# Layer norm and weight products of the node tiles moved ahead in the opening of a two-layer graph kernel

## The reference

```
h   = relu(layernorm(x))
A   = relu((adj + adj.T) / 2);  D = sum(A, axis=1);  d = D ** -0.5
x   = x + relu((I - d A d) @ (h @ W0))                 # layer 0
h   = relu(layernorm(x))
out = x + diag(adj) * (h @ W1[0]) + triu(adj, 1) @ (h @ W1[1])
        + tril(adj, -1) @ (h @ W1[2]) + bias           # layer 1
```

## Time and profile before

| | us |
|---|---|
| median of 3 runs (968.04 to 968.94) | 968.15 |
| the profiled execution | 966.95 |
| its span in the trace | 965.1 |
| first matmul of step 0 starts | 93.75 |
| PE busy | 915.6 (95% of the span) |
| DVE / ACT / POOL busy | 554.6 / 493.7 / 283.9 |

### The profile page before, as it was taken

One profiled execution on the slowest core, in us unless ns is written; L12 is line 12 of the kernel. 1 busy time (PEld: TensorE's weight loads), 2 busy tenths in 40 slices (PEclk: granted clock), 3 DMA queues, 4 the chain that ended last, 5 costly groups with the idle time before them and its releaser, 6 DMA issues.

```text
span 965.1 us, 17388 instructions
## 1 busy us (share of the span) xinstructions
PE 915.6 (95%) x4535; PEld 774.2 (80%) x4535; DVE 554.6 (57%) x1481; ACT 493.7 (51%) x1042; POOL 283.9 (29%) x284
## 2 busy tenths in 40 slices
PE   3657999999999999999999998999999999999998
PEld 2547788888888888888888887888888888888886
DVE  4896787777777776565656554543433433433442
ACT  2898466666666664555455554343333333333331
POOL 4783344344343443434434442111111100000000
PEclk9899999999999999999999999999999999999999
DMA  9996999999999985655565555676656655555552
GB/s 286 328 265 156 290 338 322 326 327 332 324 331 318 335 275 180 178 171 162 174 196 161 166 175 176 187 221 190 188 179 189 193 160 170 166 164 165 158 168 69
DMA packets 181689, 213.73 MB, mean 221 GB/s; under 512 B 13712, under 2 KB 116112, under 8 KB 179600
## 3 DMA queue, kind: packets, MB, share of 16 engines
q1 hardware_dynamic: 138928, 159.23, 54.6%
q10 hardware_dynamic: 42720, 54.01, 16.1%
HBM read 145.04 MB, written 68.16 MB: 221 GB/s over the span
## 4 chain that ended last, share of the span: by engine, by line
PE 88%; DVE 4%; ACT 2%; SPq 2%; DMA 1%; issue 1%; POOL 0%; DVEq 0%; ACTq 0%; POOLq 0%
PE psAcc L543 24%; PE psAcc L541 24%; PE psAcc L542 24%; PE psA L427 3%; PE psG L510 2%; PE psG L512 2%; PE psG L511 2%; PE psZ L469 2%; DVE sring L842 1%; DMA colb<-in_adj 1%; ACT hst L573 1%; SPq L236 1%; PE psW L396 1%; DVE n_st L797 1%; PE psW L395 1%
## 5 line engine op out<-in xcount | busy, mean ns | idle before, releaser
L607 ACT ACTIVATE Lh<-C 128x512 fp32r<-128x512 f32 x256 | 161.3, 631 | 293.4 <-PE psAcc L543 233.0
L541 PE MATMUL psAcc<-Xh,Lh 128*128 128x512 f32 x512 | 206.1, 402 | 0.7 <-DVE Xl L975 0.4
L541 PE MATMUL psAcc<-Yh,Lh 128*128 128x512 f32 x512 | 200.8, 392 | 0.0
L543 PE MATMUL psAcc<-Xh,Ll 128*128 128x512 f32 x512 | 200.7, 392 | 0.0
L542 PE MATMUL psAcc<-Xl,Lh 128*128 128x512 f32 x512 | 200.2, 391 | 0.0
L543 PE MATMUL psAcc<-Yh,Ll 128*128 128x512 f32 x512 | 200.1, 391 | 0.0
L542 PE MATMUL psAcc<-Yl,Lh 128*128 128x512 f32 x512 | 199.9, 390 | 0.0
L784 DVE TENSOR_TENSOR Ll<-C,Lh 128x512 fp32r<-128x512 f32 x128 | 90.8, 711 | 143.8 <-ACT Lh L607 143.7
L543 PEld LDWEIGHTS psAcc<-Xh,Ll 128*128 128x128 f32 x512 | 96.3, 188 | 20.8
L543 PEld LDWEIGHTS psAcc<-Yh,Ll 128*128 128x128 f32 x512 | 96.1, 188 | 20.3
L541 PEld LDWEIGHTS psAcc<-Xh,Lh 128*128 128x128 f32 x512 | 96.6, 189 | 18.8 <-issue 1.5
(11 more groups left out here) (125 smaller groups left out, 1380.4 us busy)
## 6 DMA issues: line engine op xcount, KB each, us to landing
C<-at_dram SPq DMA_DIRECT2D x128, 256.0 KB, 2.7
at_dram<-AT SPq DMA_DIRECT2D x16, 1088.0 KB, 5.5
R<-in_adj SPq DMA_DIRECT2D x64, 256.0 KB, 6.2
C<-in_adj SPq DMA_DIRECT2D x64, 256.0 KB, 5.2
s_dram<-C ACTq DMA_DIRECT2D x64, 256.0 KB, 5.0
g_dram<-g ACTq DMA_DIRECT2D x32, 512.0 KB, 3.6
C<-s_dram SPq DMA_DIRECT2D x64, 256.0 KB, 3.9
t_dram<-x ACTq DMA_DIRECT2D x32, 256.0 KB, 2.1
```

What stands on the lines that cost most here:

```text
L541: mm(acc, lh, rh[:, kd, :], start=k == 0, stop=False)
L543: mm(acc, ll, rh[:, kd, :], start=False, stop=c < L1 and k == NB - 1).then_inc(used, 1)
L607: A(Lh[:, q, :], C[:, q, :], ACT.Relu if s.c < L1 else ACT.Copy).then_inc(lhi, 1)
```

## The change

SP loads the first four node tiles between the four parts of strip 0, the weights after them, and the other twelve with strips 1 to 5 (three, three, three, two, one), each ahead of its strip. Stats, norm, turn and copy of the tiles stand in lists of their own and are placed in blocks behind chunks 3, 7, 11, 15 and 18. The turned tile is written back to `hst` instead of to four buffers. The weight products have three banks instead of two (`product0`: two of `psG` and `psZ`, the last tile in `psAcc`). The transposes of quarters 0 and 1 of step 0 stand behind chunks 35 and 37, the fourth quarter and the last three weight products behind the first quarter of step 0, and `xp` is turned at the end of step 0.

```
-        TILES_WITH = [2, 2, 2, 2, 1, 2, 1, 1, 2, 1, 0, 0, 0, 0, 0, 0]
-        TURN_AT = [8, 10, 15, 16, 21, 22, 27, 28, 31, 32, 35, 36, 37, 38, 39, 39]
-        SCALE_AT = [12, 13, 19, 20, 25, 26, 31, 32, 35, 36, 39]
+        TILES_WITH = [0, 3, 3, 3, 2, 1, 0, 0, 0, 0, 0, 0, 0, 0, 0, 0]
+        STAT_AT = [-1, 0, 1, 2, 3, 3, 3, 7, 7, 7, 11, 11, 11, 15, 15, 18]
+        MEAN_AFTER = [2, 4, 6, 8, 9, 12, 14, 15]
+        POWER_AT = [0, 2, 3, 7, 7, 11, 15, 18]
+        NORMAL_AT = [1, 1, 3, 3, 3, 3, 7, 7, 7, 7, 11, 11, 15, 15, 18, 18]
+        TURN_AT = [3, 3, 3, 3, 7, 7, 7, 7, 11, 11, 15, 15, 18, 18, 20, 20]
-        COLS_AT = [9, 16, 22, 28, 32, 36]
-        DEG_AT = [9, 17, 23, 29, 33, 37]
+        COLS_AT = [7, 15, 21, 27, 31, 35]
+        DEG_AT = [7, 15, 22, 28, 32, 36]
+        ROOT_AT = [7, 15, 21, 27, 31, 35]
+        TIMES_AT = [7, 7, 15, 15, 23, 24, 29, 30, 33, 34, 37, 38]
+        HIGH_AT = [7, 7, 15, 15, 24, 25, 30, 31, 34, 35, 38, 39]
+        LOW_AT = [8, 8, 16, 16, 26, 27, 32, 33, 36, 37]
...
-            return psZ[:, :] if j == 12 else psW[:, :] if j == 13 else psG[:, j % 2, :]
+            return psAcc[:, 1, :] if j == NB - 1 else psZ[:, :] if j % 3 == 2 else psG[:, j % 3, :]
...
+                    load_tiles([g])
                     sp.dma_start(rowb[:, 0, c], rows_v[k, :, c]).then_inc(ld_first[g], 16)
                     sp.dma_start(colb[:, 0, g * Q:g * Q + w * P].rearrange("p (j c) -> p j c", c=P),
                                  cols_v[k, :, 4 * g:4 * g + w, :]).then_inc(ld_first[g], 16)
-                    if g < TILES_WITH[0]:
-                        load_tiles([g])
+                load_weights()
...
     # times_W0, PE
-                if j == 13:
-                    pe.wait_ge(d_cols, len(GROUPS) - 1)
-                elif j != 12:
-                    done = j - 3 if j >= 14 else j - 1
-                    wait(pe, prep_hi, done)
-                    wait(pe, prep_lo, done)
+                if j < NB - 1:
+                    wait(pe, prep_hi, j - 2)
+                    wait(pe, prep_lo, j - 2)
...
     # chunk loop, PE
+                if n in (36, 39):
+                    pe.wait_ge(at_ok, 1 if n == 36 else 2)
...
+                for j in range(len(TIMES_AT)):
+                    if TIMES_AT[j] == n:
+                        times_W0(j)
                 for j in range(NB):
                     if TURN_AT[j] == n:
                         turn0(j)
+                if n in (35, 37):
+                    pe.wait_ge(p0S, 35 if n == 35 else 38)
+                    rows_T(Step(None, 0), 0 if n == 35 else 1)
+            columns0(len(GROUPS) - 1)
+            pe.wait_ge(p0S, len(CH0) - 1)
+            rows_T(Step(None, 0), 2)
             times_W0(12)
...
     # step 0, PE
-                if k == 11 and c < NB:
+                if k == (11 if c else 15) and c < NB:
...
+                    if c == 0 and q == 0:
+                        pe.wait_ge(p0S, len(CH0))
+                        rows_T(t, 3)
+                        times_W0(13)
+                        times_W0(14)
+                        times_W0(15)
...
     # chunk loop, ACT
-                for j in range(NB):
-                    if 2 * j + 6 == n:
+                for j in range(NB + 2):
+                    if j < NB and NORMAL_AT[j] == n:
                         normal0(j)
-                for j in range(NB):
-                    if TURN_AT[j] == n:
-                        turned0(j)
+                    if j >= 2 and TURN_AT[j - 2] == n:
+                        turned0(j - 2)
+                for j in range(len(HIGH_AT)):
+                    if HIGH_AT[j] == n:
                         scaled_hi(j)
...
     # chunk loop, DVE
+                stats_at(n)
+                for j in range(len(LOW_AT)):
+                    if LOW_AT[j] == n:
                         scaled_lo(j)
...
     # chunk loop, POOL
+                for e in range(len(ROOT_AT)):
+                    if ROOT_AT[e] == n:
+                        root(e)
                 for u in range(NB // 2):
-                    if 4 * u + 2 == n:
+                    if POWER_AT[u] == n:
```

More of the change, by code:

```diff
@@ L244, in load_first @@
                                  cols_v[k, :, 4 * g:4 * g + w, :]).then_inc(ld_first[g], 16)
-                    if g < TILES_WITH[0]:
-                        load_tiles([g])
+                load_weights()
             def load0(i):
                 k = NB - 1 - i
+                j = NQ + sum(TILES_WITH[0:i])
+                load_tiles(range(j, j + TILES_WITH[i]))
                 if i >= 3:
@@ L255, in load0 @@
                                  cols_v[k, :, 0:k, :]).then_inc(ld_col[i % 3], 16)
-                j = sum(TILES_WITH[0:i])
-                load_tiles(range(j, j + TILES_WITH[i]))
             def load_next(s, q):
@@ L285, in _ @@
                 load0(i)
-                if i == NB - 5:
-                    load_next(Step(None, 0), 0)
-            for q in range(1, NQ):
+                if i in (10, 12):
+                    load_next(Step(None, 0), i // 2 - 5)
+            for q in range(2, NQ):
                 load_next(Step(None, 0), q)
@@ L410, in times_W0 @@
                 pe.wait_ge(t0_ok, j + 1)
-                if j == 13:
-                    pe.wait_ge(d_cols, len(GROUPS) - 1)
-                elif j != 12:
-                    done = j - 3 if j >= 14 else j - 1
-                    wait(pe, prep_hi, done)
-                    wait(pe, prep_lo, done)
+                if j < NB - 1:
+                    wait(pe, prep_hi, j - 2)
+                    wait(pe, prep_lo, j - 2)
                 for b in range(HB):
                     f = slice(b * F, (b + 1) * F)
-                    last = mm(product0(j)[:, f], T0[j % 4][:, f], x1[:, 0, 0:F], start=True, stop=True)
+                    last = mm(product0(j)[:, f], hst[:, node(j), f], x1[:, 0, 0:F], start=True, stop=True)
                 last.then_inc(w0_ok, 1)
@@ L579, in turned0 @@
                 act.wait_ge(t0, j + 1)
-                wait(act, w0_ok, j - 3)
-                A(T0[j % 4], psAcc[:, j % 2, :], ACT.Copy).then_inc(t0_ok, 1)
+                A(hst[:, node(j), :], psAcc[:, j % 2, :], ACT.Copy).then_inc(t0_ok, 1)
             def scaled_hi(j):
@@ L827, in degrees, with stats_at @@
                                        op0=ALU.mult, op1=ALU.add).then_inc(d_safe, 1)
+            def stats_at(n):
+                for j in range(NB):
+                    if STAT_AT[j] == n:
+                        stats0(j)
+                        for u in range(NB // 2):
+                            if MEAN_AFTER[u] == j:
+                                mean0(u)
             def scaled_lo(j):
@@ L843, in _ @@
                                 rowb[:, (NB - 1 - k) % 3, 4 * g * P:4 * g * P + w], ALU.add).then_inc(p0S, 1)
[L844 to L849, removed]
                 for e in range(len(DEG_AT)):
@@ L852, in _ @@
                         degrees(e)
-                for j in range(len(SCALE_AT)):
-                    if SCALE_AT[j] + 2 == n:
+                stats_at(n)
+                for j in range(len(LOW_AT)):
+                    if LOW_AT[j] == n:
                         scaled_lo(j)
-            sum_T(Step(None, 0), 0)
+                if n in (36, 38):
+                    sum_T(Step(None, 0), 0 if n == 36 else 1)
+                if n == 38:
+                    split_lo(Step(None, 0), 0)
+            scaled_lo(10)
             degrees(len(GROUPS) - 1)
-            scaled_lo(10)
+            split_lo(Step(None, 0), 1)
             scaled_lo(11)
-            sum_T(Step(None, 0), 1)
-            split_lo(Step(None, 0), 0)
+            sum_T(Step(None, 0), 2)
             scaled_lo(12)
+            split_lo(Step(None, 0), 2)
+            sum_T(Step(None, 0), 3)
             scaled_lo(13)
-            sum_T(Step(None, 0), 2)
-            split_lo(Step(None, 0), 1)
             scaled_lo(14)
-            sum_T(Step(None, 0), 3)
+            split_lo(Step(None, 0), 3)
             scaled_lo(15)
-            split_lo(Step(None, 0), 2)
-            split_lo(Step(None, 0), 3)
             dve.wait_ge(d_inv, len(GROUPS))
```

57 lines of the change are left out of this document (16 added, 41 removed).

## The result

| | before | after | ratio |
|---|---|---|---|
| median, us | 968.1 (965.57 to 968.94, 4 runs) | 998.05 (997.36 to 999.58, 4 runs) | 1.0313 [1.0295, 1.0331] |
| span of the profiled execution | 965.1 | 997.9 | |
| step 0's first matmul | 93.75 | 122.83 | |
| from there to the end | 871.35 | 875.1 | |

The change makes the kernel 3.1% slower. The forecast was 991 us, in a range from 976 to 1000. The profiled execution, 999.58 us, is the longest of the four; the other three have spans of 995.6 to 996.6. So the trace after holds about 1.5 us that the median doesn't, and a difference between two traces can be off from that of the medians by as much.

What follows compares the result with a forecast made beforehand. ACT and DVE waits were taken to bound the opening, PE the 64 steps. Step 0 at 116 us plus 872.2 behind it gives span 988, 23 more than before; added to the median, 991 us, range 976 to 1000.

Steps and rivals of the forecast that it cites:

- the forecast's own sum: Whole kernel: step 0 starts at 109 to 119 us, so the span is 984 to 994; chance 0.62.
- the slow clock or further waits (994 to 1003): Whole kernel: half clock in step 0's first quarter, or more waits, gives 994 to 1003 us; chance 0.13.
- The weights: Start of opening: weights land behind strip 0 and four tiles, so the first chunk begins at 14.9 us, not 7.16.
- The blocks: Opening to chunk 22: waits followed block by block leave ACT idle 29.7 us and end at 93.6 us.
- The faster rival: Opening: blocks fill idle time, ACT idle only 6 us, step 0 at 85.4, time 960.6 us; chance 0.09.
- The rival with half the waits: Opening: 15 us less idle time, step 0 at 101, 976 us; case 972 to 984, chance 0.14.
- The tiles ahead of the strips: Early loads: strip 1 lands 3.9 us later, near 22.5, hidden since its first chunk is held until 36.
- The rest: From chunk 22 to step 0: 15.5 us of ACT work plus waits, step 0 taken at 116 us.
- my upper bound: Late opening: followed through degrees, ring, POOL's additions and chunk 36, step 0 starts at 118.5 us.
- The fixed part: From step 0's first matmul to the end: 2.34 us stall goes, 0.45 and 2.7 us are added, 872.2 us.
- The slow clock: Step 0's first quarter at half clock adds 2.8 us, 997 us; chance 0.13 shared with further waits.

Runs made afterwards that it cites:

- e1: The changed kernel with the two weight loads issued first, as before: 991.41 us, ratio 1.0234.
- e2: The kernel before with the two weight loads moved behind strip 0: 968.46 us, ratio 0.9994.
- e3: The changed kernel with stats, power and mean of tiles 7, 10, 11, 13, 14 and 15 one block earlier: 987.67 us, ratio 1.0197.
- e5: The changed kernel, loads and late part kept, with the chunk loop's stats, norms, turns, products and degrees back in their old places: 974.27 us, ratio 1.0057.
- e14: The changed kernel with the pairs one block earlier and the weights loaded first as well: 979.52 us, ratio 1.0112.
- e6: The changed kernel with the chunk loop's work back in its old places and the weights loaded first: 974.81 us, ratio 1.0065.
- e9: The kernel before with only the late part of the change; loads, weights and chunk-loop places as before: 967.76 us, ratio 0.9999.
- e10: The changed kernel with quarters 0 and 1 of step 0 behind the last chunk again: 997.49 us, ratio 1.0312.
- e13: The changed kernel with columns, degrees and roots of groups 3 to 5 one chunk later: 1001.58 us, ratio 1.0337.
- e4: The changed kernel with xp turned behind k = 11 of step 0 again: 1001.29 us, ratio 1.0342.
- e8: The changed kernel with xp turned behind k = 15 in step 1 too: 998.71 us, ratio 1.0315.

## Why the prediction was right, and where it was off

The measured 998.05 us lies inside the stated range, 2 us from its upper end, but above the 984 to 994 us that the forecast's own sum gave (chance 0.62). It fell in the next case, "the slow clock or further waits (994 to 1003)", which had 0.13, and by further waits. The direction, the cause and the chain through the blocks were forecast; that 998 was still inside owes something to a wide range.

**The weights.** Forecast 14.9 us for the first chunk, measured 15.23 on PE and 15.01 on ACT. That it counts nearly in full in this order is shown (e1: the relu of chunk 0 comes 8.2 us earlier, step 0 7.8 us, the median 6.6), and e2 shows that it is the order that makes it count.

**The blocks.** The chain followed held at nearly every point: `mean0` of pair 0 forecast at 23.3, measured end 23.34; end of the first block 39.4, measured 39.2; `mean0` of pair 3 at 47.2, measured 46.91; waits of ACT forecast as 5.4, 3.8, 4.8 and 3.1 us, measured as 5.44, 3.97, 5.66 and 3.53. ACT's idle time up to chunk 22, forecast as 29.7 us, is 30.8 (23.6 for the mean, 7.2 for DVE's chunks). That the late stats, power and mean of each pair's second tile cause most of these waits is shown by e3, which moves the three together; that the places as a whole are the main loss is shown by e5. The faster rival needed under 13.5 us of idle time on ACT; the waits for the mean alone are 23.6. The rival with half the waits (972 to 984) didn't hold; even e3, with the pairs in time, measured 987.67, and it took the weights first as well to come to 979.52 (e14).

**The tiles ahead of the strips.** "That is hidden, since its first chunk is held until 36": in the trace after, PE has no wait for a transfer between 16 and 100 us, so it held here, as a reading of waits and not by a run. In the old places it costs 6 to 7 us (e6 against e9). Along one order of undoing the terms are: loads ahead 6.7 (968.1 to 974.81, e6), blocks with the pairs in time 4.7 (to 979.52, e14), pairs late 11.9 (to 991.41, e1), weights late 6.6 (to 998.05). In another order they would have other sizes: the weights are worth 6.6 us here and nothing in the old places.

**The rest: the step that was off.** I took chunk 22 at 93.6 and 22.4 us from there to step 0, between bounds of 15.5 and 24.9. The relu of chunk 22 ends at 95.9, and from there it takes 26.9 us: 2.3 and 4.5 us more, and more than my upper bound. Of the 2.3, 1.1 was there when ACT's last block began (87.26, forecast 86.2). Then chunk 21 stood behind the last turns on PE at half clock, and chunk 22 waited for POOL. Of the 4.5 us behind it, about 3 are a term that I had sized too small, ACT's waits. I had given them 6.9 us beside 15.5 us of work; the view of ACT from 94 us to step 0 has

```profile
ACT sring L614 <- DVE sring L848: 10.8, 12, 2.0
```

of which about 10 lie behind chunk 22, beside about 17 us of work. DVE in turn mostly waits for PE, and for PE the views above show waits that I had not priced: 2.5 us for POOL ahead of the columns, and 1.4 us for a strip that I had "just in time". e10 and e13 show that neither the quarters between the chunks nor the columns' place can be taken out for a gain: another wait stands close behind each. So the size is measured; that its cause is a set of near ties rather than one wait is what these two runs suggest, and no run takes the whole 4.5 us away.

**The fixed part: half right.** The transposes and products behind step 0 cost about what was said: 875.1 us less the two stalls of 1.44 and 1.34 is 872.3, forecast 872.2. But the stall of 2.34 us that was to go came back as 2.78. ACT issues the next `xp` load behind the turn; in step 0 that was 13.3 us behind the first matmul (107.0), now 16.2 (139.0), and step 1 turns at k = 11 as before. I had followed `xp` to its turn and not to the load that the turn releases. e4 shows that the late turn is worth 3 us all the same, and e8 that one more late turn moves the stall by a step.

**The slow clock.** Step 0 itself started at full clock (matmuls 0.23 apart), so the rival's place was wrong; the half clock lay in the opening, at 0.50 from 84 to 94 us. What it cost there no run isolates. The Trainium skill, page TensorE: Matmul & The Clock Gate, section What's actually happening, has the throttled clock as the default that sustained activity releases. The trace agrees for the first matmuls of the span, by their times:

```profile
15.23 1.94 PE L446 MATMUL psA<-ident,colb 128*128 128x128 f32 x8 [15.23 <-DMA x<-in_L_gnn_W]
...
70.02 1.04 PE L446 MATMUL psA<-ident,colb 128*128 128x128 f32 x8
```

Eight transposes of the same size take nearly twice as long at 15.23 us. The clock column of the windows reads 1.00 for 14 to 30 us all the same, so for the first stretches of a trace the times of the rows say more than that column.

Together: 2.3 + 4.5 + 2.8 = 9.6 us, the difference between the forecast span 988.2 and 997.9 but for rounding. By the medians the forecast was 7 us short (991 against 998.05); the rest is that the traced execution was the slowest of four.

## What to carry to other kernels

Work that is moved into idle time must be moved with everything that releases it: here the data of the tiles were there early, but each pair's second tile, its power on POOL and its mean on DVE stood behind the chunks, and blocks on in-order engines turn each such lag into idle time of the busiest engine. Look at what an early load pushes back: the same late weights cost 0 or 6.6 us, and the same early tiles 6 to 7 us or, where the blocks hold the next strip anyway, nothing that a wait shows. Where a stall goes, follow the transfer that the moved instruction releases, one iteration further.

## What the runs showed of the hardware that was not expected

A stall of 2.15 us in step 0 of the kernel with `xp` at k = 11 (e4) cost more than itself. The windows of that kernel around it (stretch, length, PE, PEld, DVE, ACT, POOL, clock, DMA):

```profile
136.00:138.00 2.00, 0.00 (x0) 0.01 (x1) 0.79 (x2) 1.77 (x5) 0.17 (x1) 1.00 0.99 409
138.00:140.00 2.00, 1.99 (x9) 2.00 (x10) 0.92 (x2) 0.99 (x3) 0.00 (x0) 0.51 0.70 254
140.00:142.00 2.00, 2.00 (x7) 1.54 (x7) 1.36 (x3) 1.07 (x2) 0.00 (x0) 0.64 0.55 191
142.00:144.00 2.00, 2.00 (x13) 1.65 (x12) 1.27 (x4) 0.70 (x2) 0.00 (x0) 1.00 1.16 263
```

After the gap the granted clock is half, 1.2 GHz, from 138.0 to about 141.4 us: the turn's four transposes take 1.08 us instead of 0.60, and the next matmuls start 0.42 apart instead of 0.23. Less its stall, the stretch from step 0 to the end is 874.4 us here and 872.3 in the change: 2.1 us more, of which half of these 3.4 us, 1.7, would be the clock (an estimate from these times). The stall of 2.34 us before the change was followed by full clock:

```profile
105.00:107.00 2.00, 1.50 (x11) 1.44 (x12) 0.69 (x1) 1.24 (x3) 0.00 (x0) 1.00 1.04 413
107.00:109.00 2.00, 2.00 (x11) 1.63 (x10) 1.46 (x3) 1.20 (x3) 0.00 (x0) 1.00 0.77 210
```

So two gaps of nearly the same length at the same place of step 0 had different prices, and a stall of PE is better priced with a possible half clock behind it.

The small operations of DVE beside POOL, 1.23 us in the earlier trace rows (four numbers a partition there, not eight), were as costly in the degrees, with only two numbers a partition:

```profile
42.58 1.18 DVE L823 SCALAR_TENSOR_TENSOR dsafe<-d 128x2 f32<-128x2 f32 x1
...
71.06 1.18 DVE L823 SCALAR_TENSOR_TENSOR dsafe<-d 128x2 f32<-128x2 f32 x1
```

The rows before have 0.87 us for a group's whole degrees up to the next chunk; here one of its four operations takes 1.18 us, since the block form puts it beside POOL's four additions (40.02 to 44.43 us). The statistics at 43.68, beside the same additions, took 0.86 us as in the earlier trace rows, so of the stats only the small variance operation was held (0.99 us at 19.36, ending with POOL's first addition).
